# A fused recurrent and mixture-of-experts block: the turn between its two halves reordered, router batches regrouped, twelve slot buffers, and the last seven slot tiles in steps of one

## The reference

```
xn   = layernorm(x)                                   # over the last axis
hg   = xn @ W_hg                                      # 128 -> 512
hidden, gate = split(hg)                              # 256 each
h[t] = (1 - z[t]) * h[t-1] + z[t] * (relu(hidden[t]) + 0.5),  z = sigmoid(gate)   # written in logs in the reference
s    = h @ W_out                                      # 256 -> 128
shared = (silu(xn @ Sg) * (xn @ Su)) @ Sd
probs  = softmax(xn @ Wr);  top 2 experts of each token, with their probabilities as weights
routed = sum over the two experts e of  w_e * ((silu(xn @ Wg[e]) * (xn @ Wu[e])) @ Wd[e])
out  = x + s * silu(routed + shared)
```

## Time and profile before

| | |
|---|---|
| time, median of 3 runs | 320.56 us (319.11 to 321.23) |
| the profiled execution | 320.5 us, of which the span of its instructions is 318.8 us |
| busy share of the span | PE 93%, DVE 79%, ACT 74%, POOL 63% |
| mean granted clock of PE | 0.975 |
| idle time of PE between its first and last matmul that a wait explains | 3.5 us at the turn, 1.1 us in iteration 6, under 1 us at every other place |

### The profile page before, as it was taken

The page is one execution under the profiler, slowest core; times in us unless marked ns, Lnnn a source line. Parts: engine busy times, 40 slices in busy tenths (PEclk is TensorE's granted clock), DMA queues, the critical chain, the costliest instruction groups (busy, mean ns, idle before and its releaser), DMA issues.

```text
span 318.8 us, 6032 instructions
## 1 busy us (share of the span) xinstructions
PE 296.4 (93%) x1537; PEld 201.4 (63%) x1537; DVE 252.6 (79%) x659; ACT 236.1 (74%) x505; POOL 202.0 (63%) x239
## 2 busy tenths in 40 slices
PE   8999999998999999999789999999999999999920
PEld 3566776775566766666475675676767767676620
DVE  6999999999999999898805775877777877777830
ACT  1678999998998478987746876878778787878510
POOL 7578546630168677787866777777565665656570
PEclk9999999999999999999959999999999999999995
DMA  7937999959126775343895436675665555550000
GB/s 224 288 93 331 399 450 404 442 203 434 54 86 241 221 253 202 128 152 127 290 397 193 155 105 201 167 235 157 190 187 159 165 155 135 163 155 29 16 0 0
DMA packets 28272, 63.62 MB, mean 200 GB/s; under 512 B 3733, under 2 KB 22688, under 8 KB 27472
## 3 DMA queue, kind: packets, MB, share of 16 engines
q1 hardware_dynamic: 20928, 45.45, 42.0%
q0 software_dynamic: 6752, 17.06, 14.3%
q10 hardware_dynamic: 560, 0.73, 0.7%
HBM read 29.32 MB, written 35.14 MB: 202 GB/s over the span
## 4 chain that ended last, share of the span: by engine, by line
PE 39%; POOL 17%; DVE 17%; issue 14%; DMA 9%; ACT 1%; POOLq 1%; DVEq 0%; ACTq 0%; SPq 0%
PE p_u L1032 17%; POOL slots L365 13%; PE p_s L1057 9%; DMA slots<-arena,pos 7%; PE p_sh L1044 4%; PE p_u L960 4%; DVE stats L556 3%; DVE rec L589 2%; PE p_xt L1008 2%; POOL out L371 2%; PE p_s L971 2%; DVE meanvar L562 1%; DVE rec L595 1%; DMA arena<-slots 1%; DVE prod L603 1%
## 5 line engine op out<-in xcount | busy, mean ns | idle before, releaser
L371 POOL DMA_INDIRECT out<-arena x83 | 82.2, 991 | 43.0 <-DVE arena L848 25.3
L960 PE MATMUL p_u<-xT,w_front 128*128 128x512 f32 x192 | 89.2, 598 | 1.9 <-DVE prod L603 1.1
L365 POOL DMA_INDIRECT slots<-arena,pos x64 | 72.9, 1138 | 27.2 <-issue 16.5
L1032 PE MATMUL p_u<-arena 128*128 x166 | 78.2, 593 | 0.0
L1057 PEld LDWEIGHTS p_s<-arena,rec 128*128 128x128 f32 x332 | 43.3, 191 | 21.6 <-issue 21.6
L960 PEld LDWEIGHTS p_u<-xT,w_front 128*128 128x128 f32 x192 | 33.8, 190 | 33.1 <-issue 31.6
L822 DVE TENSOR_TENSOR rec<-p_u,rec 128x512 f32<-128x512 f32 (+1 forms) x42 | 28.8, 685 | 31.1 <-ACT rec L492 31.1
L499 ACT ACTIVATE rec<-p_sh 128x512 f32<-128x512 f32 (+1 forms) x42 | 24.8, 591 | 29.4 <-PE p_sh L1044 29.4
L1057 PE MATMUL p_s<-arena,rec 128*128 x332 | 44.2, 276 | 1.3 <-ACT rec L499 1.3
L1032 PEld LDWEIGHTS p_u<-arena 128*128 128x128 f32 x166 | 28.3, 190 | 19.6 <-issue 19.6
L595 DVE TENSOR_TENSOR_SCAN rec<-rec 128x512 f32<-128x512 f32 x32 | 39.3, 1227 | 1.1
(11 more groups left out here) (135 smaller groups left out, 439.6 us busy)
## 6 DMA issues: line engine op xcount, KB each, us to landing
slots<-arena SPq DMA_DIRECT2D x4, 4116.0 KB, 26.8
arena<-slots SPq DMA_DIRECT2D x41, 392.0 KB, 3.5
arena<-in_W_lines SPq DMA_DIRECT2D x2, 2304.0 KB, 10.5
arena<-in_x SPq DMA_DIRECT2D x15, 256.0 KB, 5.1
arena<-in_W_lines SPq DMA_DIRECT2D x4, 768.0 KB, 4.6
out<-arena POOLq DMA_INDIRECT x83, 2.6
slots<-arena,pos POOLq DMA_INDIRECT x64
w_front<-in_W_front ACTq DMA_DIRECT2D x1, 392.0 KB, 5.3
```

The costliest lines, as they stand in the source:

```text
L365: pool.indirect_dma_start(slots, index, xrow[:, t], None).then_inc(s_disp[t % WINDOW], 16)
L371: pool.indirect_dma_start(out, index, xg[:, n % RX, h, X], None, bounds_check=T - 1, oob_is_err=False)\
L960: nc.tensor.matmul(p_u[:, n % 4], w_front[:, UPS[q]:UPS[q] + P], xT[:, c % XB], start=True, stop=True)\
L1032: last = nc.tensor.matmul(p_u[:, n % 2 * 2 + h], xsT[:, n % 2, h * P:(h + 1) * P], w_lines[:, bass.DynSlice(line_at[2 * n + h], 4 * P)], s ...
```

## The change

- **Router batches.** BATCHES goes from seven, of 12, 8, 8, 8, 4, 12 and 12 tiles, to four, of 20, 16, 4 and 24; they run in iterations 2, 4, 5 and 10. `ln_stats` of the later chunks are dealt out anew. The last logits move from iteration 9 to 8, and the third `positions` part of the first group from 8 to 9.
- **Exponentials.** On ACT they move from behind `normalise` at the end of iterations 5 and 11 to between `rec_in` and `shared_silu` of iterations 6 and 12. DVE does `key_bases(0)` ahead of `probabilities(0)`.
- **Block weights** of the second group go from POOL to DVE (`late_weights`, iteration 13).
- **The turn.** `load_keys(0)` moves into iteration 15, `tile_keys(0)` into iteration 12; PE does `rec_down(15)` first, then `slot_transpose(0)`, then `shared_down(15)`. The buffers `xs` and `xsT` now lie in the space of the scans.
- **Loads.** The eight late weight lines come one by one, every second one behind two more dispatches. `load_slots` 4 to 9 wait until step n-4 is normalised. RX goes from 10 to 12.
- **Steps.** 38 steps of two tiles and then seven of one (45 steps instead of 42).

```diff
-RX = 10
+RX = 12
+SINGLES = 7
+AHEAD = 4
+    WIDTHS = [2] * ((USED - SINGLES) // 2) + [1] * SINGLES
-    BATCHES = [(0, 12), (12, 20), (20, 28), (28, 36), (36, 40), (40, 52), (52, 64)]
+    BATCHES = [(0, 20), (20, 36), (36, 40), (40, 64)]
...
-        STATS = {1: [6, 7], 2: [8, 9], 3: [10, 11, 12], 4: [13, 14], 5: [15]}
+        STATS = {1: [6, 7, 8, 9], 2: [10], 3: [11, 12, 13, 14], 4: [15]}
...
+                if AHEAD <= n < PAIRS0:
+                    sp.wait_ge(s_xs, n - AHEAD + 1)
                 if n >= RX:
-                    sp.wait_ge(s_out[n % RX], 32 * (n // RX))
+                    sp.wait_ge(s_out[n % RX], 16 * sum(width(k) for k in range(n % RX, n, RX)))
...
-                part = slice((OWN_LINES + k * LATE) * LINE, (OWN_LINES + (k + 1) * LATE) * LINE)
-                sp.dma_start(w_lines[:, part], W_lines[:, part]).then_inc(s_lines, 16)
+                for line in range(OWN_LINES + k * LATE, OWN_LINES + (k + 1) * LATE):
+                    if line % LATE:
+                        for j in range(WINDOW // 2):
+                            sp.wait_ge(s_disp[j], 16 * (k + 2))
+                    part = slice(line * LINE, (line + 1) * LINE)
+                    sp.dma_start(w_lines[:, part], W_lines[:, part]).then_inc(s_lines, 16)
...
-            block_weights(1)
             pool.wait_ge(s_w4, 2)
...
+                if i == 6:
+                    exponentials(0)
+                if i == 12:
+                    exponentials(1)
                 if i == NCH - 1:
                     copy_down(i - 1)
                     normalise_slots(0)
...
-                if i == 5:
-                    exponentials(0)
-                if i == 11:
-                    exponentials(1)
...
+            def late_weights():
+
+                nonlocal steps
+                a, b, n = TILES[1].start, TILES[1].stop, len(TILES[1])
+                weights = p01[:, :, a:b].rearrange("p k (t w) -> p k t w", w=1).to_broadcast([P, 2, n, BLOCK])
+                dve.wait_ge(s_p01, 2)
+                nc.vector.tensor_tensor(eq4[:, :, 0:n], eq4[:, :, 0:n], weights, ALU.mult).then_inc(s_step, 1)
+                steps += 1
+                dve.wait_ge(s_step, steps)
+                nc.vector.tensor_tensor(xrow[:, a:b, W4:W4 + BLOCK], eq4[:, 0, 0:n], eq4[:, 1, 0:n], ALU.add).then_inc(s_w4, 1)
...
                 if i == 10:
-                    route_top(6)
-                    route_second(6)
+                    route_top(3)
+                    route_second(3)
...
-                if 6 <= i <= 8:
-                    positions(0, i - 6)
-                if i == 9:
+                if i in (6, 7, 9):
+                    positions(0, (i - 5) // 2 if i > 7 else i - 6)
+                if i == 8:
                     copy_logits(LATE_LOGITS)
                 if i == 12:
+                    tile_keys(0)
                     probabilities(1)
                 if 13 <= i <= 14:
                     positions(1, i - 13)
+                if i == 13:
+                    late_weights()
...
+                if i == NCH - 1:
+                    load_keys(0)
                 up(i, 4)
                 up(i, 5)
...
-            load_keys(0)
+            rec_down(NCH - 1)
             slot_transpose(0)
-            rec_down(NCH - 1)
             shared_down(NCH - 1)
             slot_transpose(1)
             gate_up(0)
```

More of the change, by code:

```diff
@@ L171, in recurrent_moe_block @@
         i01 = sb("i01", [P, 2, NT], U32)
-        k_a, k_b, k_c, k_d, k_e = (sb(f"k_{n}", [P, TG], U32) for n in "abcde")
         key = sb("key", [P, NT], U32)
@@ L189, in recurrent_moe_block @@
         fresh = sb("fresh", [P, LINES])
-        TP = max(b - a for part in PARTS for a, b in part)
+        TP = max(max(b - a for part in PARTS for a, b in part), -(-TB * E // LINES))
         moved = sb("moved", [P, LINES, TP])
         ptmp = sb("ptmp", [P, LINES, TP])
+        k_a, k_b, k_c, k_d, k_e = (ptmp.rearrange("p l t -> p (l t)")[:, n * TG:(n + 1) * TG].bitcast(U32) for n in range(5))
         eq = moved.rearrange("p l t -> p (l t)")[:, 0:TB * E].rearrange("p (t e) -> p t e", e=E)
@@ L372, in store_out, with first_weights @@
                         .then_inc(s_out[n % RX], 16)
-            def block_weights(g):
-                t = TILES[g]
-                a, b, n = t.start, t.stop, len(t)
-                pool.wait_ge(s_p01, g + 1)
-                weights = p01[:, :, a:b].rearrange("p k (t w) -> p k t w", w=1).to_broadcast([P, 2, n, BLOCK])
-                nc.gpsimd.tensor_tensor(eq4[:, :, 0:n], eq4[:, :, 0:n], weights, ALU.mult).then_inc(s_spot, 1)
-                pool.wait_ge(s_spot, g + 1)
-                nc.gpsimd.tensor_tensor(xrow[:, a:b, W4:W4 + BLOCK], eq4[:, 0, 0:n], eq4[:, 1, 0:n], ALU.add).then_inc(s_w4, 1)
+            def first_weights():
+                b = len(TILES[0])
+                pool.wait_ge(s_p01, 1)
+                weights = p01[:, :, 0:b].rearrange("p k (t w) -> p k t w", w=1).to_broadcast([P, 2, b, BLOCK])
+                nc.gpsimd.tensor_tensor(eq4[:, :, 0:b], eq4[:, :, 0:b], weights, ALU.mult).then_inc(s_spot, 1)
+                pool.wait_ge(s_spot, 1)
+                nc.gpsimd.tensor_tensor(xrow[:, 0:b, W4:W4 + BLOCK], eq4[:, 0, 0:b], eq4[:, 1, 0:b], ALU.add).then_inc(s_w4, 1)
             for c in range(HEAD + 2, NCH):
                 rstd_of(c)
-            block_weights(0)
+            first_weights()
             pool.wait_ge(s_w4, 1)
@@ L906, in _ @@
                     positions(1, i - 13)
-            for g in range(2):
-                tile_keys(g)
+                if i == 13:
+                    late_weights()
+            tile_keys(1)
             for n in range(PAIRS):
@@ L989, in prefix @@
                     pe.wait_ge(s_const, CONSTS)
-                pe.wait_ge(s_lgc, NCH if g else EARLY_LOGITS)
+                pe.wait_ge(s_lgc, NCH if g or k == 2 else EARLY_LOGITS)
                 if g or k:
@@ L1017, in load_keys @@
                 for h in range(width(n)):
-                    tile = 2 * n + h
+                    tile = first_tile(n) + h
                     line_at[tile] = nc.tensor.value_load(toff[tile:tile + 1, g:g + 1], min_val=0, max_val=(LINES - 1) * LINE)
@@ L1032, in gate_up @@
                     last = nc.tensor.matmul(p_u[:, n % 2 * 2 + h], xsT[:, n % 2, h * P:(h + 1) * P],
-                                            w_lines[:, bass.DynSlice(line_at[2 * n + h], 4 * P)], start=True, stop=True)
+                                            w_lines[:, bass.DynSlice(line_at[first_tile(n) + h], 4 * P)], start=True, stop=True)
                 last.then_inc(s_gu, 1)
@@ L1089, in _ @@
                     logits(read(i))
-                if i in (7, 8):
-                    prefix(0, i - 6)
+                if i == 7:
+                    prefix(0, 1)
+                if i == 8:
+                    logits(LATE_LOGITS)
                 if i == 9:
-                    logits(LATE_LOGITS)
-            load_keys(0)
+                    prefix(0, 2)
+            rec_down(NCH - 1)
             slot_transpose(0)
-            rec_down(NCH - 1)
             shared_down(NCH - 1)
```

31 lines of the change are left out of this document (15 added, 16 removed).

## The result

The changed kernel takes **317.33 us** (median of 6 runs, 317.03 to 319.04) where the kernel before takes 320.69 us (6 runs, 318.95 to 321.23): a ratio of **0.9911, 95% interval 0.9886 to 0.9937**. The forecast was 315.6 us. The span of the profiled execution fell from 318.8 to 315.6 us, by 3.2 us, where the sum had 4.9.

A forecast was written before the change was run, and what follows sets the result against it. PE, busy 93% of the span, was taken as the bound, so savings count only where it waits, its clock is low, or behind its last matmul. Terms -0.2 +3.1 +1.5 -5.4 -1.3 -3.1 +0.5 = -4.9 us: 315.6 us, range 311.0 to 318.4.

The forecast's parts named there:

- within 1%: Outcome class for the whole kernel: time within 1%, 3.2 us, of no change; chance 0.19.
- faster by more: Outcome class for the whole kernel: faster by more than 1%, 3.2 us; chance 0.76.
- iterations 5 and 6: Regrouped batches remove PE's 1.1 us wait; moved exponentials add one of 0.9 to 1.0 us: net -0.2 us (-0.6 to +0.6).
- batch in iteration 10 and the clock behind it: DVE's longer chain makes PE wait, +3.1 us (2.5 to 3.6); low clock behind it, +1.5 us (0 to 2.6).
- turn: Between front and second half: the 3.5 us wait and low clock go, -5.4 us (-6.1 to -3.3).
- step 10: Second half: with twelve buffers its load waits only for the last dispatch, rows come in time: -1.3 us (-1.4 to 0).
- single steps and the end: Seven steps of one tile: shorter tail, -3.1 us, against slower pace, +0.5 us (0 to 2).
- Rival A: Iteration 10: the batch of 24 stays hidden, its wait and low clock stay away: 311.0 us; chance 12%.
- Rival B: POOL's dispatches do not get faster, step 10 costs 1 to 2 us again: 317.5 us; chance 14%.
- 6.3 us against 10.8 us: At the end: time from the last `gate_up` to its store, forecast against the kernel before.
- Rival C: Single steps at the end bound by latency, 2.75 us a step instead of 1.63: 322.9 us, slower; chance 4%.
- a sign of being wrong: Single steps at the end: the forecast called itself wrong if steps of one take more than 1.9 us.

The follow-up runs named there:

- e2_exps_back: The changed kernel with the exponentials back at the end of iterations 5 and 11, behind the normalisations: 317.97 us.
- e1_batch_in_9: The changed kernel with the batch of 24 tiles moved from iteration 10 to the start of iteration 9 on DVE: 313.29 us, ratio to before 0.9753.
- e4_turn_alone: The kernel before with only the order at the turn changed, still ten buffers, old batches and pairs to the end: 322.34 us, ratio 1.0028.
- e3_ten_buffers: The changed kernel with ten slot buffers in place of twelve, nothing else: 318.76 us.
- e11_turn_twelve: e4_turn_alone with twelve slot buffers in place of ten, and the memory moved that makes room for them: 319.1 us, ratio 0.9951.
- e6_eleven_singles: e1_batch_in_9 with the last eleven tiles one at a time in place of seven: 312.59 us.
- e10_last_rows_apart: e6_eleven_singles with the last two tiles' final operations on DVE done one tile after the other: 311.60 us.
- e9_batch_ten_buffers: e1_batch_in_9 with ten slot buffers in place of twelve: 315.70 us.
- e7_loads_not_spaced: e1_batch_in_9 with SyncE's loads of late weights and slots not spaced: 312.31 us.

## Why the prediction was right, and where it was off

The direction and most of the terms were right, but the gain was over-stated: 3.4 us by the medians where 4.9 were forecast. 317.33 us lies at the upper edge of the forecast's own band (313.4 to 317.3), and a ratio of 0.9911 is the outcome "within 1%", to which 0.19 was given, not "faster by more", 0.76. By the timeline of the changed kernel against the rows of before, last store to last store:

| step | forecast | measured | from |
|---|---|---|---|
| iterations 5 and 6 | -0.2 | -0.5 | `rec_down(9)` 112.48, before 113.02 |
| batch in iteration 10 and the clock behind it | +4.6 | +5.4 | last `up` 160.27, before 155.44, less the line above |
| turn | -5.4 | -5.4 | 170.81 - 160.27 against 171.35 - 155.44 |
| step 10 | -1.3 | -1.2 | `gate_up(12)` 203.60, before 205.29 on the timeline |
| single steps and the end | -2.6 | -1.5 | 307.26 - 203.60 against 310.45 - 205.29 |
| sum | -4.9 | -3.2 | 307.26, before 310.45 |

**Iterations 5 and 6.** The new wait is 1.15 us (0.9 to 1.0 forecast), the net term -0.5, inside its bounds. The regrouped batches gave more than the 1.1 us of the wait: `rec_down(5)` starts at 74.91 in place of 76.51. The wait for `shared_gated(5)` is gone also in e2_exps_back, where the exponentials stand as before. What I had not seen is that leaving the exponentials where they were would have cost more, 1.83 us for `shared_gated(6)`. The Trainium skill ("ScalarE: Activation LUTs", What ACT_TABLE_LOAD costs) has a drain of about as much again with each load, by which the wait would have been some 3.7 us, an estimate. Both loads in the rows take 1.28 us, with the next activation directly behind, so the trace does not agree here.

**The batch of 24.** The mechanism, the place and the length of DVE's chain were right (13.28 us). The wait came out at 3.48 us against 3.1, inside the bounds, and the clock cost 1.63 against 1.5. The rest of the 5.4 is that a wait costs PE more than its length: from `rec_down(9)` to `rec_down(10)` it takes 124.03 - 112.48 = 11.55 us where 120.85 - 113.02 = 7.83 stood before, 3.72 us for a wait of 3.48. Rival A, the batch hidden, did not come; e1_batch_in_9 shows that one iteration earlier it is hidden.

**The turn** was right to 0.1 us, twice over: in the changed kernel and in e4_turn_alone. The register loads cost PE nothing in iteration 15: from `rec_down(14)` to the last two `up` it takes 160.27 - 157.59 = 2.68 us, as in the kernel before (155.44 - 152.76).

**Step 10.** The forecast price was right, and that was in part luck. Spacing the loads should "remove 2 to 5 us" of POOL's waits for landing: they fell from 6.3 to 3.0 us in the changed kernel, but were 4.4 to 7.5 us in the spaced kernels built on e1_batch_in_9 and 6.2 in the one without spacing, so the 3.0 can't be put down to it. The last dispatch should end "20 to 22 us behind the last `up`", with "1 to 3 us to spare"; it ended 185.08 - 162.04 = 23.0 us behind it. The load of step 10 took 3.9 us to land, at 191.8, and this is the moment at which ACT took the rows, with nothing to spare (the timeline of SP, then that of ACT):

```profile
187.91 0.36 SPq L282 DMA_DIRECT2D arena<-slots  x1
191.82 0.88 ACT L487 ACTIVATE rec<-arena 128x128 f32<-128x128 f32 x2
```

Twelve buffers brought little here, some 0.3 us by the estimate at e3_ten_buffers. What kept PE from waiting is that it came to the turn 4.8 us later: e11_turn_twelve has the same buffers and its last dispatch at 184.11, the changed kernel at 184.12, and only the first, whose PE comes early, waits, 2.95 us. That does not make the batch's loss a price worth paying. In the seven kernels with the batch in iteration 9 and twelve buffers PE comes 3.7 to 5.6 us earlier and still does not wait, because the last dispatch begins earlier as well (179.64 to 181.79): the batch in iteration 10 had held up DVE's `late_weights` too, and with it POOL, whose first dispatch behind it starts at 151.44 in the changed kernel and at 147.72 in e1_batch_in_9. Rival B, dispatches not faster, is nearly what happened (1.0 us earlier), and it cost nothing only because PE came that much later.

**The end is the step that was mis-sized**: "6.3 us against 10.8 us" was 7.5 against 10.8. I wrote that "POOL's 1.3 us a store keeps up". It keeps up with PE's 1.63 us a step, but that is not the pace at which rows become ready where pairs give way to singles. The lag between a tile's `gate_up` and its rows shrinks there, so rows come faster than PE starts tiles: the rows of the last pairs are ready at 290.36, 292.71 and 294.78, 2.35 and 2.07 us apart, and each pair is two stores of 1.3 us. The rows of the first single are ready at 296.31 and their store begins at 299.03, 2.7 us behind; POOL stores back to back (0.30 us between two) to the last and makes up only part of it. The forecast's reading of the end before was off as well: when the last rows were ready there (307.24), not six other stores stood ahead of theirs but three, of which one had begun (306.48, 307.87, 309.16). And the order at the end of DVE's list makes the last two tiles ready 0.5 us apart, whatever the queue holds. e6_eleven_singles took the first cause away and gained nothing, e10_last_rows_apart the second as well, and the tail fell to 301.61 - 294.92 = 6.7 us. The second alone, with seven singles, was not tried; by the rows of the changed kernel it would have brought nothing, since the last store but one (305.97) already begins 0.30 us behind the one ahead of it, whenever its rows come. Rival C, single steps bound by latency, did not come: single `gate_up` are 1.5 to 2.4 us apart, the widest at the first of them (288.27 to 290.64), behind which the work of the pairs is still being done. Their mean, (299.75 - 288.27) / 6 = 1.91 us, just passes the 1.9 us that the forecast gave as a sign of being wrong; but that sign was set too low, for from `gate_up(12)` to the last `gate_up` it takes 1.8 us more than before (96.15 against 94.36), where the forecast had 1.4 + 0.5 = 1.9.

## What to carry to other kernels

Price a saved wait against the next fixed arrival on the same engine: 5.4 us saved at the turn were worth nothing alone and 1.6 us with more buffers; nothing was lost at the arrival only where the engine came late for another reason, or where the dispatches came earlier too. A batch that is wider saves per-instruction time on its engine and lengthens the one chain it stands in; ask which iteration has the slack for the whole of it, not how much the engine saves in all. At the end of a pipeline, look at when the last results become ready, not at the mean pace: the last store waits for the one ahead of it, and a queue must be empty before the order of the last two counts.

## What was not expected of the hardware

PE's granted clock fell to 0.50, the 1.2 GHz level, with waits of 2.95 (e11_turn_twelve), 3.48 (the changed kernel), 3.49 (e2_exps_back), 3.53 (e3_ten_buffers) and 5.54 us (e4_turn_alone), not with one of 2.29 (e9_batch_ten_buffers, 1.00 in 190 to 194). But the same wait did not bring the same low stretch. In the changed kernel the clock was still 1.00 in 123 to 124, when PE had started again, and 0.55 in 124 to 125; in e3_ten_buffers it was 0.71 in 122 to 123, while PE still stood, and stayed at 0.50 to 129. `rec_down` and `shared_down` took 4.31 us in the one and 129.67 - 124.93 = 4.74 us in the other, with the two pieces of the `up` ahead of them at 1.10 and 2.04 us. From `rec_down(9)` to `rec_down(11)` it was 21.01 and 22.40 us, 21.05 in e2_exps_back, and 15.66 in the kernel before: one and the same wait of 3.5 us cost 5.4 us twice and 6.7 us once.

And once, in e1_batch_in_9, the clock fell while the rows show PE busy throughout, behind the late logits (24 pieces of matmul of 16 columns). The next `rec_down` then stood at 105.97, in e7_loads_not_spaced at 104.29, and of these 1.7 us 1.1 were left at the last `up`. The profiles of ten other kernels with those matmuls in the same place kept 1.00. What set it off in that run stays open.
